# A decoder layer on one core: a shared burst of value products, a norm chain by columns, five banks for the late products

## The reference

```
x = x + attention(layernorm(x)) @ w_o.T + b_o       # 32 query heads, 8 key/value heads, head size 32, rope, causal
x = x + fake_quant(layernorm(x)) @ fake_quant(ctx)  # (512 x 1024) @ (1024 x 1024) per batch, 8 bit steps
x = x + layernorm(x) @ W_org.T + sum_e coeff_e * (layernorm(x) @ lora_down_e) @ lora_up_e
```

## Time and profile before

| | |
|---|---|
| median of three runs | 717.89 us |
| profiled execution | 717.73 us, span 715.9 us, mean granted clock 0.976 |
| PE busy | 660.2 us (92%), 4512 matmuls and transposes |
| DVE, ACT, POOL busy | 430.2 us (60%), 424.7 us (59%), 281.2 us (39%) |
| DMA | 93.46 MB, mean 131 GB/s |
| value products (L947) | 1280, in 64 bursts |
| loads of the first group's queries | 2, 6.3 us from issue to landing (median) |

### The profile page before, as it was taken

The page is one execution under the profiler, slowest core; times in us unless marked ns, Lnnn a source line. Parts: engine busy times, 40 slices in busy tenths (PEclk is TensorE's granted clock), DMA queues, the critical chain, the costliest instruction groups (busy, mean ns, idle before and its releaser), DMA issues.

```text
span 715.9 us, 12713 instructions
## 1 busy us (share of the span) xinstructions
PE 660.2 (92%) x4512; PEld 530.3 (74%) x4512; DVE 430.2 (60%) x1137; ACT 424.7 (59%) x1025; POOL 281.2 (39%) x301
## 2 busy tenths in 40 slices
PE   4996899999999899999989699999999698999998
PEld 3985677898777678777756577777878576788886
DVE  6796677875877634677676966442326788811122
ACT  5425678878787747599977675755315782611320
POOL 2046645534444354455320720506715024814520
PEclk9998999999999999999999899999999989999999
DMA  7646854752555733225561340505326352614102
GB/s 264 227 152 187 244 164 124 213 149 76 144 159 160 201 87 99 94 56 150 178 181 60 100 130 1 147 1 156 124 75 234 100 187 82 189 47 117 44 16 102
DMA packets 43934, 93.46 MB, mean 131 GB/s; under 512 B 5505, under 2 KB 5889, under 8 KB 42433
## 3 DMA queue, kind: packets, MB, share of 16 engines
q1 hardware_dynamic: 34416, 66.45, 29.3%
q0 software_dynamic: 3696, 15.73, 9.5%
q10 hardware_dynamic: 5760, 10.49, 4.0%
HBM read 72.72 MB, written 19.92 MB: 129 GB/s over the span
## 4 chain that ended last, share of the span: by engine, by line
PE 72%; DVE 12%; ACT 6%; issue 4%; POOL 4%; DMA 1%; ACTq 0%; DVEq 0%
PE dense L1040 47%; PE probt L932 8%; PE score L920 5%; PE pv L947 5%; POOL w_lo L1653 2%; DVE stats L1333 2%; ACT prob_all L1131 2%; DVE xres L1435 2%; PE score L1040 1%; DVE w_lo L1269 1%; PE misc L956 1%; PE probt L901 1%; ACT w_hi L1084 1%; PE misc L986 1%; PE misc L901 1%
## 5 line engine op out<-in xcount | busy, mean ns | idle before, releaser
L1040 PE MATMUL dense<-w_hi,act_t 128*128 128x512 f32 (+1 forms) x684 | 226.0, 391 | 5.4 <-POOL act_t L1664 1.8
L1289 DVE CUSTOM_DVE_ANT_0 prob_all<-score,mask_sb 128x128 f32<-128x128 f32 (+3 forms) x256 | 123.2, 488 | 121.0 <-PE score L920 119.1
L1653 POOL TENSOR_TENSOR w_lo<-stage,w_hi 128x512 fp32r<-128x512 f32 x85 | 110.1, 1303 | 201.8 <-ACT w_hi L1084 201.6
L1131 ACT ACTIVATE prob_all<-prob_all,neg_max 128x128 f32<-128x128 f32 (+3 forms) x256 | 142.7, 558 | 37.4 <-DVE neg_max L1289 36.0
L1040 PEld LDWEIGHTS dense<-w_hi,act_t 128*128 128x128 f32 x684 | 128.5, 193 | 28.4 <-issue 3.8
L1040 PE MATMUL dense<-act_t,w_hi 128*128 128x512 f32 x408 | 138.2, 420 | 3.3 <-DVE xres L1435 2.1
L1040 PE MATMUL dense<-w_lo,act_t 128*128 128x512 f32 (+1 forms) x372 | 135.5, 385 | 1.6 <-ACT w_lo L1089 1.4
L932 PE MATMUL probt<-ident_sb,prob_all 128*128 128x128 f32 x640 | 113.7, 277 | 5.1 <-ACT prob_all L1140 4.5
L1084 ACT ACTIVATE w_hi<-stage 128x512 fp32r<-128x512 f32 x117 | 72.0, 623 | 45.6 <-PE dense L1040 34.8
L1140 ACT ACTIVATE prob_all<-probt 128x128 f32<-128x128 f32 (+3 forms) x160 | 68.5, 428 | 47.8 <-PE probt L932 47.0
L932 PEld LDWEIGHTS probt<-ident_sb,prob_all 128*128 128x128 f32 x640 | 80.0, 142 | 22.0 <-issue 7.5
(11 more groups left out here) (168 smaller groups left out, 858.7 us busy)
## 6 DMA issues: line engine op xcount, KB each, us to landing
q_stack<-rope_dram POOLq DMA_DIRECT2D x15, 768.0 KB, 7.3
stage<-in_w_qk SPq DMA_DIRECT2D x40, 256.0 KB, 3.0
rope_dram<-act_t ACTq DMA_DIRECT2D x40, 256.0 KB, 2.5
stage<-in_w_o SPq DMA_DIRECT2D x32, 256.0 KB, 2.9
stage<-in_ctx_kv SPq DMA_DIRECT2D x24, 256.0 KB, 3.4
stage<-in_w_org SPq DMA_DIRECT2D x24, 256.0 KB, 3.1
xres<-in_x SPq DMA_DIRECT2D x8, 512.0 KB, 7.0
prob_all<-in_x SPq DMA_DIRECT2D x8, 512.0 KB, 5.9
```

The lines of the kernel that those rows point to most:

```text
L1040: last = engine.matmul(dst, lhs, rhs, start=(k == 0 and c == 0), stop=(k == g.kts - 1 and c == len(pairs) - 1))
L1131: engine.activation(prob[:, u % P_SLOTS, 0:length], prob[:, u % P_SLOTS, 0:length], ACT.Exp, bias=neg_max[:, m:m + 1], scale=-1.0, accum_o ...
L1289: engine.tensor_tensor_reduce(prob[:, u % P_SLOTS, 0:length], score_bank[u % 2][:, 0:length], mask_sb[:, S - length:S], -1.0, HIGHEST, ALU ...
L1653: engine.tensor_tensor(slot_lo(p, 0, NW), raw_of(p), slot_hi(p, 0, NW).bitcast(F32), ALU.subtract).then_inc(g_piece, 1)
```

## The change

Four things change.

The value products of query tiles 0 and 1 of a group are issued in one burst at the group's slot 12; the burst of slot 8 is gone. `t_pv` counts three bursts per group instead of four. The transposed probabilities of both tiles share one of the six slots: tile 0 has columns 0 to 127 and tile 1 columns 128 to 383.

The first two operations of the norm chain of batch 1 are written column by column, eight operations on 128x1 elements in place of two on 128x4. The constants are computed at slot `HEAD - 3` instead of `HEAD + 2`. The turns and low copies of batch 1's tokens are three slots later; the normalisations stay.

The chain of the third norm of batch 1, tile 1, is on POOL instead of DVE.

From the first output tile of batch 1 on, dense tiles go round five banks: the two dense ones, the two score banks and the value bank, which no unit uses any more. A tile waits for the one five before it. The first tiles in the score and value banks wait for all maxima and scalings.

```
+BURSTS = (0, 1), (2,), (3,)
+DENSE_BANKS = 5
+WIDE_FROM = "out", 1, 0, 0
-CHAINS_ON_VECTOR = [... for t in range(NT)] + [(3, 1, 1), (3, 1, 3)]
+CHAINS_ON_VECTOR = [... for t in range(NT)] + [(3, 1, 3)]
...
+        self.bank_no, self.tile_before, last = [], [], {}
+        wide = self.tile_no[WIDE_FROM]
+        for no in range(len(self.tiles)):
+            self.bank_no.append(no % 2 if no < wide else (no - wide) % DENSE_BANKS)
+            self.tile_before.append(last.get(self.bank_no[no]))
+            last[self.bank_no[no]] = no
...
-                at = HEAD + 17 + 4 * t + 2 * half
+                at = HEAD + 20 + 4 * t + 2 * half
...
-        dense_bank = [bank("dense0"), bank("dense1")]
+        dense_bank = [bank("dense0"), bank("dense1")] + score_bank + [pv_bank]
...
+        def place(u):
+            gi, i, h = unit(u)
+            return GROUP * (len(BURSTS) * gi + max(i - 1, 0)) + h
+
+        def turned_to(u, a, b):
+            start = P if unit(u)[1] == 1 else 0
+            return prob_t[:, place(u) % PROBT_SLOTS, start + a:start + b]
...
-            def values(w):
+            def values(gi, tiles):
...
+                for i in tiles:
+                    for h in range(GROUP):
+                        e.wait_ge(*probt_done((gi * NT + i) * GROUP + h))
+                if 0 in tiles and gi:
                     e.wait_ge(v_attn, gi)
+                for i in tiles:
+                    e.wait_ge(*evacuated("v", b, 0, i))
+                    for c in range(i + 1):
+                        for h in range(GROUP):
+                            last = engine.matmul(
+                                pv_bank[h * HD:(h + 1) * HD, i * P:(i + 1) * P], values_sb[:, b, c, g * HD:(g + 1) * HD],
+                                turned_to((gi * NT + i) * GROUP + h, c * P, (c + 1) * P), start=(c == 0), stop=(c == i))
...
-                    dst = dense_bank[no % 2][:, 0:g.width]
-                    if k == 0 and no >= 2:
-                        e.wait_ge(*tile_done(no - 2))
+                    dst = dense_bank[plan.bank_no[no]][:, 0:g.width]
+                    if k == 0 and plan.tile_before[no] is not None:
+                        e.wait_ge(*tile_done(plan.tile_before[no]))
+                    elif k == 0 and dst_is_units(no):
+                        e.wait_ge(v_max, UNITS)
+                        e.wait_ge(v_attn, GROUPS)
...
-                if u >= PROBT_SLOTS:
-                    e.wait_ge(t_pv, (u - PROBT_SLOTS) // GROUP + 1)
+                if place(u) >= PROBT_SLOTS:
+                    e.wait_ge(t_pv, (place(u) - PROBT_SLOTS) // GROUP + 1)
...
-                ln(engine.tensor_scalar(w, var, EPS, -ROOT_SCALE, ALU.add, ALU.mult))
+                for t in range(NT):
+                    ln(engine.tensor_scalar(w[:, t:t + 1], var[:, t:t + 1], EPS, -ROOT_SCALE, ALU.add, ALU.mult))
                 wait_ln()
-                ln(engine.tensor_scalar(ln_i[:, :], w.bitcast(I32), -0.5, RSQRT_SEED, ALU.mult, ALU.add))
+                for t in range(NT):
+                    ln(engine.tensor_scalar(ln_i[:, t:t + 1], w[:, t:t + 1].bitcast(I32), -0.5, RSQRT_SEED, ALU.mult, ALU.add))
...
+                if j == HEAD - 3:
                     constants()
```

More of the change, by code:

```diff
@@ L58 @@
 TERMS = 3
-CHAINS_ON_VECTOR = [(which, b, t) for which, b in ((1, 0), (1, 1), (2, 1)) for t in range(NT)] + [(3, 1, 1), (3, 1, 3)]
+CHAINS_ON_VECTOR = [(which, b, t) for which, b in ((1, 0), (1, 1), (2, 1)) for t in range(NT)] + [(3, 1, 3)]
 EARLY_LAGS = 2.0, 3.5, 4.5, 6.0, 9.5
@@ L415, in ready @@
         no = self.tile_no.get((g.kind, g.b, g.nb, n), 0)
-        if k == 0 and no >= 2:
-            before, tile = self.tiles[no - 2]
+        if k == 0 and self.tile_before[no] is not None:
+            before, tile = self.tiles[self.tile_before[no]]
             if not self.past(j, ("evac", before.kind, before.b, before.nb, tile), 1):
@@ L1063, in tensor_program @@
                     step(s)
-                if 0 <= u - PV_LAG < UNITS and (u - PV_LAG) % GROUP == GROUP - 1:
-                    values((u - PV_LAG) // GROUP)
+                if 0 <= u - PV_LAG < UNITS:
+                    gi, i, h = unit(u - PV_LAG)
+                    for tiles in BURSTS:
+                        if (i, h) == (tiles[-1], GROUP - 1):
+                            values(gi, tiles)
                 for gi in ends_at(u, PV_LAG):
@@ L1184, in down_high @@
                 e.wait_ge(v_route, ROUTE_OPS * (b + 1))
-                engine.activation(act_t[LORA_T[b]][:, 0, m, :], dense_bank[no % 2][:, :], ACT.Copy,
+                engine.activation(act_t[LORA_T[b]][:, 0, m, :], dense_bank[plan.bank_no[no]][:, :], ACT.Copy,
                                   scale=coef_rows[:, m:m + 1]).then_inc(a_down, 1)
@@ L1295, in take_out_turned @@
                 e.wait_ge(t_turned, u + 1)
-                if u >= PROBT_SLOTS:
-                    e.wait_ge(t_pv, (u - PROBT_SLOTS) // GROUP + 1)
-                engine.tensor_copy(prob_t[:, u % PROBT_SLOTS, 0:length],
+                if place(u) >= PROBT_SLOTS:
+                    e.wait_ge(t_pv, (place(u) - PROBT_SLOTS) // GROUP + 1)
+                engine.tensor_copy(turned_to(u, 0, length),
                                    probt_bank[u % 2][:, 0:length]).then_inc(v_probt, 1)
@@ L1417, in rotate @@
                 kind, b, nb = plan.ropes[m]
-                src = dense_bank[plan.tile_no[kind, b, nb, 0] % 2] if m >= 2 else score_bank[m]
+                src = dense_bank[plan.bank_no[plan.tile_no[kind, b, nb, 0]]] if m >= 2 else score_bank[m]
                 c = nb if kind == "q" else NKV + nb
@@ L1442, in take_out_tile @@
                 g, n, _ = plan.steps[s]
-                src = dense_bank[plan.tile_no[g.kind, g.b, g.nb, n] % 2]
+                src = dense_bank[plan.bank_no[plan.tile_no[g.kind, g.b, g.nb, n]]]
                 cols = slice(g.nb * NW, (g.nb + 1) * NW)
```

24 lines of the change are left out of this document (7 added, 17 removed).

## The result

The kernel with the change takes 714.32 us (median of 8 runs, 711.60 to 716.28) against 718.30 us for the kernel before (8 runs, 716.67 to 720.65): ratio 0.9937, 95% interval 0.9921 to 0.9954, some 4.5 us gained by the ratio (4.0 by the medians). I had forecast 704.3 us and a range from 698 to 712. The sign and the places are right; two thirds of the sum are missing.

A forecast was written before the change was run, and what follows sets the result against it. PE was taken to bound the kernel (72% of the chain that ended last, DVE 12%). Front 4.0, attention 5.6 and tail 4.0 summed to 13.6 us off, giving 704.3 us, range 698 to 712.

The forecast's parts named there:

- constants: Front: computing the constants at slot 5, where POOL is idle, brings all later DVE work 1.6 us earlier.
- columns: Front, norm chain: column operations escape the POOL port lock but the next operation waits instead; 0 us gained.
- turns later: Front: moving batch 1's turns three slots shortens one PE stall by 1.5 us and removes another of 0.95.
- shared bursts: Attention: each of 16 bursts saved spares PE 0.33 us, some counted half; 4.6 us.
- wait for the scaling: Attention: PE's wait for DVE's scaling, moved from slot 8 to 12, goes; 1.6 us less new maxima waits, 1.0 net.
- banks, first stall: Tail: five banks remove PE's 2.75 us bank wait at 572.15; ACT is late next, so 2.0 us is kept.
- banks and chain, second stall: Tail: the 2.82 us wait at 603.90 goes; the token-sums turn moves by 2.0 plus 1.95 us from the chain leaving DVE.
- the wait at 85.84 stays as it is: Front: PE's 2.14 us wait for a take-out on ACT at 85.84 us was expected to remain.
- Rival A: Front held by ACT and POOL from 66 to 85 us; 3 of 4 us come back, 707.3 us; chance 0.15.
- The counted half: Attention, four groups between 350 and 450 us: PE waits for others anyway, so burst savings there count half.
- rival B: Attention paced by ACT: closed PE gaps reopen as probability waits, 4 of 5.6 us lost, 708.3 us; chance 0.12.
- DVE has no pause there: Tail, before the token-sums turn at 614.11: DVE works without pause, so the turn moves only by 2.0 and 1.95 us.

The follow-up runs named there:

- experiment 5: The kernel before with only the constants moved five slots earlier on DVE; 717.35 us, ratio 0.9982 to the kernel before.
- experiment 10: The change with turns at their old slots and the value scaling cut to one column in 512 (timing only); 712.11 us, ratio 0.9902.
- Experiments 7: The change with turns at their old slots, and each group's value scaling and its copies one slot later; 720.76 us, ratio 1.003.
- experiment 12: The change with turns at their old slots, scaling behind the next maximum and take-out on DVE except groups 7 and 15; 717.17 us, ratio 0.9976.
- experiment 3: The kernel before with only the tail's edits, five banks and one norm chain on POOL; 718.21 us, ratio 0.9993.
- experiment 4: The change with batch 1's turns back at their old slots; 713.02 us, ratio 0.9939 to the kernel before.

## Why the prediction was wrong

The largest misses are the shared bursts, 4.6 us forecast and 1.7 in the traces, and the later turns, whose 2.45 us came at the first score and were mostly lost by the first inverse sums. Steps of the prediction, in us; "at the place" is read from traces, "in the time" from medians.

| step | forecast | at the place | what the runs showed |
|---|---|---|---|
| constants | 1.6 | 1.95 | right; experiment 5: 1.3 in the time |
| columns | 0 | 0.4 | the lock as forecast, a little gained |
| turns later | 2.45 | +1.2 to 2.5, then -1.1 to -1.6 | wrong |
| shared bursts | 4.6 | 1.7: 0.33 in 6 groups, 0.5 in one, -0.2 in 5 | price right, count wrong |
| wait for the scaling | 1.0 | 0 | moved onto the maximum behind it |
| banks, first stall | 2.0 | 1.84 | right, with ACT last as forecast |
| banks and chain, second stall | 1.95 more | 1.0 more | size off |
| the way from there to the end | 0 | -0.9 | not forecast |

**The turns.** The step "the last two half turns now stand among the first units; no wait at this distance" failed. I looked at the banks that they share with the transposes and not at the queues behind a turn: DVE's low copies stand in front of the first maxima (1.50 us) and of the transposes (1.44), and in front of each stands ACT's high copy. The last one starts at 79.44 us, 4.4 us behind its turn (75.06), behind an exponential that had waited for a maximum. And 1.77 us at 69.67 is the same turns meeting ACT's rope work: the low copy before it waited 4.63 us for ACT. The forecast was right up to the first score, 4.3 forecast and 3.7 measured, and then it stopped reading. That "the wait at 85.84 stays as it is" was wrong as well: it is gone, in exchange for the two. Rival A named this stretch and ACT, not DVE; no run took work from either, so their shares are not shown.

**The bursts.** "Between 350 and 450 us PE waits for others anyway, there I count half" was the right question at the wrong scale. PE busy 49.74 of 50 us says that PE is the bound over 50 us, not at each of a group's 16 slots. The first tile's burst stood where DVE has the scaling beside a maximum; while PE did the burst, DVE could catch up. Taken away, it leaves a wait: waits for maxima doubled, and experiment 10 brought them back to their old size by taking the scaling away. That gave 1.4 of the 1.8 us missing in groups 1 to 7, so this cause is shown there. The counted half of groups 11 to 13, and the 0.2 us lost in group 8, have no experiment of their own. That rival B's engine, ACT, holds it is true for smaller waits, 0.4 us before and 1.1 with the change, of which 0.44 hung on the scaling too.

**The scaling's wait.** It went from PE's burst to PE's score. The work that PE waits for hadn't become earlier, only the instruction that waits had moved, and on DVE the next maximum stood behind the same scaling. Experiments 7 and 12 show that another order on DVE is worse.

**The tail.** The first 2.0 came as 1.84. At the token sums DVE's corrections took 1.57, 0.94 and 1.53 us, since they are now beside POOL's low pieces (before 1.25, 0.94 and 0.75): the earlier start ran into another engine's work. That is 1.1 us more, as much as is missing of the 3.95, but the account has other terms. "DVE has no pause there" was wrong: between 587 and 595 us it had stood 1.5 us in four waits for PE, which are gone now. And its first correction step starts only 3.10 us earlier (587.47, now 584.37), 0.3 more than the tail's first turn and not 1.84.

Then PE stands 5.2 us in one piece, and the products behind it run partly at 1.2 GHz. That is what took 0.9 back: the eight transposes at 608.44 take 1.88 us to the next product, the same at 614.37 take 0.79, and the three products behind them 1.30 in place of 0.78; although the 0.48 us of waiting that stood in it is gone, this stretch is 0.89 longer than before, and from the next turn to the end both kernels take the same (93.18 and 93.15 us). From 608.4 to 611.6 us the clock was 0.52. In all seven profiles with this tail it is 0.5 to 1.95 us shorter than before from the first turn to the end, 1.3 in the mean, where four profiles with the old tail agree within 0.02 (153.46 to 153.48); in the time 0.5, whose interval takes in the 1.3. No run held the clock fixed, so what the tail would gain without it isn't shown.

**The range.** The lower bounds of the parts were 1, 1.5 and 0, in sum 2.5: 715.4 us. The range ended at 712 because I took at most two rivals together. The turns and the bursts had the same flaw, priced without the queue of the engine that was just in time, and in the tail the waits and the clock behind the new stall were left out, so all three fell short together.

## What to carry to other kernels

Where the order on every engine is fixed, time saved on the busiest engine counts only up to the next instruction of another queue that was just in time. Before pricing such a saving, read who would be late at that very slot, not the busy share over the stretch, and add the waits that the saved time had been hiding. A wait that is "removed" by moving the waiting instruction comes back at the next one that needs the same engine's queue; and where several gains rest on one assumption, the range has to hold the case that all of them fail.

## What the runs showed of the hardware

- The port shared by DVE and POOL works as a lock also for moved work: the same DVE subtraction (L1299) takes 0.69 us alone and 1.76 us in experiment 12, L1444 0.75 and 1.57 us. In experiment 12 L1299 ended 0.55 us behind POOL's operation (207.73). An instruction that is moved can meet another operation of POOL and take longer.
- Two kernels with the same front start the first score up to 1.3 us apart (77.11 to 78.41 us over four profiles), so a single pair of profiles can't settle a step of that size. Between such places traces agree far better: in the five profiles with four bursts the way over groups 1 to 7 is the same within 0.07 us.
- The granted clock behind a stall differs from execution to execution: from 57 to 66 us 0.62, 0.81 and 1.00 were seen, from 82 to 89 us 0.76 and 1.00, which costs 1.4 to 1.6 us, and the mean over the runs was 0.974 before (29 runs) and 0.978 with the change (8 runs). The Trainium skill's page "TensorE: Matmul & The Clock Gate", section "What's actually happening", says that a monitor of how busy the array is sets it to full or half rate; the rows here agree on the two levels: from 611.8 to 615 us of experiment 3 the clock was 0.50, from 77.8 to 102 us of experiment 4 it was 1.00.
